# One more group of edges picked by matmul in a two-layer graph network, with its source table loaded earlier

## The chip, the core and the metric

The kernel runs on one core of one Trainium2 chip. The metric is the device time of one execution in microseconds (us); less is better. The engines named below are TensorE (PE, with its weight loads as PEld), VectorE (DVE), ScalarE (ACT), GpSimd (POOL) and SyncE (SP), which issues most of the transfers.

## What is computed

Two graph layers with a residual and a layer norm each, over 3125 nodes of 128 features and 100000 edges sorted by destination. Cut to what matters:

```python
edge_index = jnp.stack([src, dst])
x = layernorm(x + L0(x, edge_weight, src, dst, ...))
x = layernorm(x + L1(x, edge_index, ...))
# L0: msgs = z[dst] @ Wd + z[src] @ Ws + edge_weight * ww + bm
#     agg  = segment_max(msgs, dst);  hidden = relu(z @ W1a + agg @ W1b + b1);  out = hidden @ W2 + b2
# L1: two mean-aggregating layers: mean(x[src] over dst) @ Wl.T + bl + x @ Wr.T, relu between
```

The work around the change is the gather `z[src] @ Ws`, that is, for each edge one row of the table `zs = x @ Ws`, and the running maximum over the edges of one destination.

## The kernel before

The edges are cut into superbatches of 256 and the superbatches into 196 groups of two (512 edges). A loop over slots runs on all engines at once; group k enters in slot k, and its later steps are done in slots k+1 and k+2. A first stretch (about 40 us) loads the inputs, makes `zs` (stored to DRAM as `zs_d`) and the tables of keys.

In slot k, for a usual group:
- POOL runs `gathers(g)` ahead of the slots (line 1089): four indirect DMAs of 128 rows of `zs_d` each, into a ring of GR = 4 groups. Before it starts group g it waits until PE has transposed group g-4 (`t_ps`, line 1097), which frees the ring place.
- PE, `rows_T(g)` (line 1657): a matmul of nine rows for the weights of the edges (line 1663, it needs `wp_d`'s transfer of line 525), then four transposes of the gathered rows (line 1675, they need the gather's landing) into the same bank. Then `adjacent(k-2)` (lines 1724, 1727, 1735) and `products(k-1)` (line 1714).
- DVE: `scan` (line 1286), the running maximum with a mask that SP brings (line 528), and the one-hot tables of the two superbatches (lines 1269 to 1271).
- ACT: copies of the results into the adjacency table `adj` and into `aggT` (lines 896, 897) and of the transposed maxima (line 902).
- SP: `load_edges(k)` (line 521): the wp transfer after `t_ps` has reached k-1, the mask after scan k-2 is done (two buffers each), then four small row transfers of `own_rows` (line 586) and others. All of it is on one queue, in program order.

Twelve groups, PICKS, are not gathered: POOL skips them (line 1090), and PE forms their rows as a product of the whole source table with one-hot columns. For a pick (g, a) the 25 blocks h of the table are spread over slots a to g-1 (`hots`, line 129). For each h, `pick_rows` (line 1821) does two matmuls of 512 columns (line 1833), one for each of the two float32r parts, `zs_high` and `zs_low`. The one-hot columns of three blocks in four are made by ACT (lines 949 and 957), those of the fourth by DVE (line 1352). In its own slot the group needs the nine-row matmul alone (line 1661). The key row of a pick is loaded by SP in slot a-4 (`load_key`, line 588) and made float by ACT in slot a-2 (line 942).

The table itself is brought into SBUF once, in four pieces: `load_sources(n)` on SP in the slots SOURCE_SLOTS (three of 512 KB, line 602, and one of 26.5 KB, line 600), then `high_part` on ACT (line 938) and `low_part` on DVE (line 1345) in the slots that stand in SPLITS. The first pick before is group 28, worked on from slot 19.

Constants of the part that changes:

```python
PICKS = ((28, 19), (37, 28), (46, 37), (55, 46), (66, 55), (77, 66), (88, 77), (99, 88), (110, 99), (121, 110), (132, 121), (143, 132))
SPLITS = ((11, 0, 8), (13, 8, 16), (15, 16, 24), (16, 24, NT))
SOURCE_SLOTS = (8, 10, 12, 13)
```

Of the kernel before, what the change touches and what calls it, by code (L numbers as in the profile page):

```python
# [9 lines left out]
NT = -(-N // P)  # L10
# [37 lines left out]
MOST = 18  # L48
CR = 8
WIDE = 8  # L50
PICKS = ((28, 19), (37, 28), (46, 37), (55, 46), (66, 55), (77, 66), (88, 77), (99, 88), (110, 99), (121, 110), (132, 121), (143, 132))
PICKED = tuple(g for g, _ in PICKS)
SPLITS = ((11, 0, 8), (13, 8, 16), (15, 16, 24), (16, 24, NT))
SOURCE_SLOTS = (8, 10, 12, 13)
HOTS = 4
RAWS = 3
ROW = AW // 2
# [14 lines left out]
def turn(t):  # L72
    return NG if t == NT - 1 else last_group(t)
# [55 lines left out]
def hots(k):  # L129
    return [(i, h) for i, (g, a) in enumerate(PICKS) if a <= k < g  # L130
            for h in range(NT * (k - a) // (g - a), NT * (k - a + 1) // (g - a))]
# [22 lines left out]
def gnn_kernel(nc, x, src, dst, w, Wm, bm, W1, b1, W2, b2, W1lT, b1l, W1rT, W2lT, b2l, W2rT, out):  # L154
# [19 lines left out]
    with ctx:  # L174
# [3 lines left out]
        def sem(name):  # L178
            return ctx.enter_context(nc.semaphore(name))

        def carve(base, *shapes):

            at, views = 0, []
            for dt, *dims in shapes:
# [54 lines left out]
        zs_r = [nc.alloc_sbuf_tensor_at(f"zs_r{n}", [P, (h1 - h0) * ROW], f32r, offset=adj_at + 4 * h0 * ROW)[:, :]  # L239
                .rearrange("p (h n) -> p h n", n=ROW) for n, (_, h0, h1) in enumerate(SPLITS)]  # L240
        zs_high = [z[:, :, high_at:low_at] for z in zs_r]
# [134 lines left out]
        l_zs, zs_high_sb, zs_low_sb = sem("l_zs"), sem("zs_high_sb"), sem("zs_low_sb")  # L376
        l_part = [sem(f"l_part{n}") for n in range(len(SPLITS))]
        l_key, key_float = sem("l_key"), sem("key_float")
# [58 lines left out]
        def tiled(table, t, m):  # L437
            return table[t * P:(t + m) * P, :].rearrange("(t p) f -> p t f", p=P)
# [4 lines left out]
        def tiles(k, off, late=0):  # L443
            return [t for t in range(NT) if turn(t) + off + (late if t >= NT - 2 else 0) == k]
# [27 lines left out]
        def _(sp):  # L472
# [28 lines left out]
            for c in range(BB):  # L501
                n = BLAST if c == BB - 1 else P
# [18 lines left out]
            def load_edges(g):  # L521
                n, i = edges(g), g % MR
                if g >= WR:
                    sp.wait_ge(t_ps, g - WR + 1)
                sp.dma_start(wp9[:, g % WR, 0:n], wp_d[:, 512 * g:512 * g + n]).then_inc(l_wp[g % WR], 16)
                if g >= MR:
                    sp.wait_ge(scanned, g - MR + 1)
                sp.dma_start(mask[:, i, 0:n], mask_d[0:1, 512 * g:512 * g + n].broadcast_to([P, n])).then_inc(l_mask[i], 16)
# [9 lines left out]
            def usual():  # L538
                def load_quad(n, stored):
                    _, _, h0, h1, _ = PIECES[LOADS[n]]  # L540
                    if n >= 2:
                        sp.wait_ge(piece_ps, LOADS[n - 1])
                    sp.wait_ge(x1_st, 32 * stored)
                    sp.dma_start(quads[n % 2][:, 0:h1 - h0, :], tiled(parts_d, h0, h1 - h0)).then_inc(l_quad[n % 2], 16)

                def load_tile(t):
                    if t >= 2:
                        sp.wait_ge(y_sb, t - 1)
                    sp.dma_start(x_rows(t)[0:size(t), :], x[t * P:t * P + size(t), :]).then_inc(l_xr[t % 2], 16)

                def store_scale(j):
                    sp.wait_ge(scale_sb, j + 1)
                    n, w = strips(j)
                    rows = degree_rows(j)[0:32 * n:32, 0:w]
                    sp.dma_start(scale_d[0:1, span(j)[0]:span(j)[1]].rearrange("o (q c) -> (o q) c", c=w), rows).then_inc(scale_st, 16)

                def store_x1(t):
                    k = size(t)
                    sp.wait_ge(x1_sb, t + 1)
                    sp.dma_start(x1_d[t * P:t * P + k, :], hid(t)[0:k, :]).then_inc(x1_st, 16)  # L560
                    if t < NT - 2:
                        sp.wait_ge(parts_sb, t + 1)
                        sp.dma_start(parts_d[t * P:t * P + k, :], pt[0:k, :, :].rearrange("p a f -> p (a f)")).then_inc(x1_st, 16)

                def store_zr(t):
                    k = size(t)
                    sp.wait_ge(zr_sb, t + 1)
                    sp.dma_start(zr_d.rearrange("(a p) n -> p a n", p=P)[:, :, t * P:t * P + k], zr_of(t)[:, :, 0:k]).then_inc(zr_st, 16)
# [3 lines left out]
                def own_rows(k):  # L572
                    for i, g in enumerate(OWN):
                        at = (4 * g + 3) * P
                        if k == g - STEP - 2:
                            if i >= 2:
                                sp.wait_ge(t_ps, OWN[i - 2] + 1)
                            sp.dma_start(own_r[:, i % 2, 0:P], src[at:at + P].rearrange("(o e) -> o e", o=1)).then_inc(l_own_r, 16)
                        for r in range(max(0, (k - g + STEP) * ROWS), min(P, (k - g + STEP + 1) * ROWS)):
                            if r == 0:  # L580
                                sp.wait_ge(l_own_r, 16 * (i + 1))
                            if r % LOAD == 0:
                                nodes[:] = nc.values_load_multi_w_load_instructions(
                                    own_r[:, i % 2, r:r + LOAD], engines=[mybir.EngineType.SP], min_val=0, max_val=N - 1,
                                    skip_runtime_bounds_check_because=NODES)[1]
                            sp.dma_start(own[r:r + 1, i % 2, :], zs_d[bass.ds(nodes[r % LOAD], 1), :]).then_inc(l_own[i % 2], 16)

                def load_key(i):
                    g = PICKED[i]
                    if i >= 2:  # L590
                        sp.wait_ge(far_made, made_by(by_scalar, NT * (i - 1)))
                        sp.wait_ge(hot_vec, made_by(by_vector, NT * (i - 1)))
                    row = src[512 * g:512 * g + 512].rearrange("(o a e) -> o a e", o=1, e=P)
                    sp.dma_start(keys[i % 2].bitcast(i32), row.broadcast_to([P, 4, P])).then_inc(l_key, 16)

                def load_sources(n):
                    _, h0, h1 = SPLITS[n]
                    sp.wait_ge(wc_sb, 1)
                    if h1 == NT:
                        sp.dma_start(zs_raw[0:LASTN, h0, :], zs_d[h0 * P:N, :]).then_inc(l_part[n], 16)  # L600
                    else:
                        sp.dma_start(zs_raw[:, h0:h1, :], tiled(zs_d, h0, h1 - h0)).then_inc(l_part[n], 16)

                for k in range(NG + 5):
                    if 2 <= k < NG:
                        load_edges(k)
                    if k == 5:
                        sp.wait_ge(wp_st, 48 * (BB - 1))
                        sp.wait_ge(zs_st, 16 * NX)
                    if k in SOURCE_SLOTS:  # L610
                        load_sources(SOURCE_SLOTS.index(k))
                    for i, (g, a) in enumerate(PICKS):
                        if k == a - 4:
                            load_key(i)
                    own_rows(k)
                    for t in tiles(k, 0):
                        load_tile(t)
                    for t in tiles(k, 12):
                        store_x1(t)
                    for t in tiles(k, 16):  # L620
                        store_zr(t)
                    if k - 2 in DEGREE_SLOTS:
                        store_scale(DEGREE_SLOTS.index(k - 2))
                    for n, c in enumerate(LOADS):
                        if PIECES[c][0] - 1 == k:
                            load_quad(n, len([t for t in range(NT) if turn(t) + 12 <= k]))
# [185 lines left out]
        def _(act):  # L812
# [70 lines left out]
            def usual():  # L883
# [84 lines left out]
                for k in range(SLOTS):  # L968
# [7 lines left out]
                    if slots(k, 1) is not None:  # L976
                        messages(k - 1)
                    for n, (at, h0, h1) in enumerate(SPLITS):
                        if at == k:
                            high_part(n, h0, h1)  # L980
                    for i, (g, a) in enumerate(PICKS):
                        if k == a - 2:
# [182 lines left out]
        def _(dve):  # L1165
# [97 lines left out]
            def usual():  # L1263
# [90 lines left out]
                for k in range(SLOTS):  # L1354
# [23 lines left out]
                    if k - 1 in DEGREE_SLOTS[:6]:  # L1378
                        scale_from(DEGREE_SLOTS.index(k - 1))
                    for n, (at, h0, h1) in enumerate(SPLITS):  # L1380
                        if at == k:
# [223 lines left out]
        def _(pe):  # L1605
# [103 lines left out]
            def usual():  # L1709
# [111 lines left out]
                def pick_rows(i, h):  # L1821
                    u, n = NT * i + h, size(h)
                    if h == 0:
                        pe.wait_ge(zs_low_sb, len(SPLITS))
                        if i:
# [219 lines left out]
```

## Time and profile before

| | |
|---|---|
| median of 3 runs | 1096.47 us (1095.42 to 1099.88) |
| profiled execution | 1098.6 us, of which its span 1096.8 us |
| PE busy | 1020.9 us (93%) |
| DVE busy | 852.8 us (78%) |
| POOL busy | 739.7 us (67%), 701 gathers from `zs_d` among it |
| ACT busy | 671.0 us (61%) |
| mean granted TensorE clock | 0.98 |

Times in the views are microseconds from the start of the span. Busy times of POOL leave out the time in which it issues. The slots of the loop run from about 40 to 960 us; what follows (the second layer's aggregation) is PE work. Which slot a moment belongs to is read off PE: every slot k below 196 has one nine-row matmul, of line 1663, or of line 1661 where group k is picked.

### The profile page before, as it was taken

The numbers are of one execution on the slowest core, as the hardware profiler recorded it, in microseconds if no ns is written. First come the engines' busy times: TensorE is split into PE (matmuls) and PEld (weight loads), VectorE is DVE, ScalarE is ACT, GpSimd is POOL, SyncE is SP. The second block draws the span as 40 slices with busy tenths as digits, with TensorE's granted clock in tenths as the row PEclk, the third lists the DMA queues.
The fourth block names the chain that finished last, engine by engine and source line by source line (L and its number), as shares of the span: only waits on it lengthen the run. The fifth ranks groups of instructions, "written<-read, shape, count | busy, mean of one in ns | idle before, by whom it ended". The sixth has DMA issues, their size and how long they took to land.

```text
span 1096.8 us, 25699 instructions
## 1 busy us (share of the span) xinstructions
PE 1020.9 (93%) x7183; PEld 756.1 (69%) x7183; DVE 852.8 (78%) x2994; ACT 671.0 (61%) x1741; POOL 739.7 (67%) x782
## 2 busy tenths in 40 slices
PE   4898989999999999999999999998988989899997
PEld 4576667777777777776767777766666666657786
DVE  6598788888878878887979888987877877645465
ACT  3345778988887778877867887433233333313664
POOL 7767777777777777777777777777777777201332
PEclk9898999999999999999999999999999999999999
DMA  8654434344334434434444443543444353545321
GB/s 204 166 130 114 96 98 103 94 100 119 95 102 106 107 104 107 101 94 128 107 102 92 104 94 98 144 107 88 115 132 104 101 148 99 147 127 164 80 59 42
DMA packets 130203, 121.29 MB, mean 111 GB/s; under 512 B 24126, under 2 KB 115573, under 8 KB 130053
## 3 DMA queue, kind: packets, MB, share of 16 engines
q1 hardware_dynamic: 103624, 70.53, 24.5%
q0 software_dynamic: 23328, 47.82, 18.0%
q10 hardware_dynamic: 3101, 1.21, 0.5%
q8 instruction: 62, 1.02, 0.4%
q14 instruction: 88, 0.72, 0.3%
HBM read 105.60 MB, written 13.88 MB: 109 GB/s over the span
## 4 chain that ended last, share of the span: by engine, by line
PE 48%; POOL 27%; issue 13%; ACT 4%; DVE 3%; DMA 2%; ACTq 2%; DVEq 0%; SPq 0%
POOL area L1100 27%; PE bank L1833 9%; PE bank L1735 8%; PE bank L1959 7%; PE bank L1724 5%; PE bank L1802 4%; PE bank L1675 4%; PE bank L1714 3%; PE bank L1663 2%; PE bank L1924 2%; ACT area L949 1%; PE bank L1910 1%; DMA area<-zs_d,area 1%; ACT hot_r L957 1%; ACTq L889 1%
## 5 line engine op out<-in xcount | busy, mean ns | idle before, releaser
L1100 POOL DMA_INDIRECT area<-zs_d,area x701 | 679.7, 970 | 216.4 <-issue 210.9
L896 ACT CAST adj_w<-bank 128x325 f32 x391 | 176.6, 452 | 312.7 <-PE bank L1735 244.7
L1286 DVE TENSOR_TENSOR_SCAN area<-area,bank 128x512 f32<-128x512 bf16 x196 | 249.6, 1274 | 141.1 <-PE bank L1675 122.2
L1270 DVE TENSOR_SCALAR area<-area 128x325 bf16<-128x325 f16 x782 | 252.2, 323 | 0.0
L1735 PE MATMUL bank<-area 128*128 128x104 f32 x1564 | 225.1, 287 | 0.2
L1269 DVE TENSOR_SCALAR area<-area 128x128 bf16<-128x128 f16 x782 | 209.3, 268 | 5.4 <-PE bank L1735 5.3
L1735 PEld LDWEIGHTS bank<-area 128*128 128x128 f32 x1564 | 196.1, 197 | 10.6 <-issue 2.0
L1833 PE MATMUL bank<-hot_r,zs_r 128*128 128x512 f32 x600 | 176.1, 420 | 1.9 <-ACT hot_r L957 1.2
L1724 PE MATMUL bank<-area 128*128 128x325 bf16 x782 | 151.5, 307 | 9.8 <-DVE area L1271 5.4
L949 ACT ACTIVATE area<-adj_w,node_c 128x512 bf16<-128x512 f32 x225 | 156.5, 744 | 0.0
L1675 PE MATMUL bank<-ident,area 128*128 128x128 f32 x706 | 117.1, 289 | 27.5 <-DMA area<-zs_d,area 27.1
L957 ACT ACTIVATE hot_r<-area 128x512 fp32r<-128x512 bf16 x225 | 133.2, 639 | 1.1
L1675 PEld LDWEIGHTS bank<-ident,area 128*128 128x128 f32 x706 | 74.6, 141 | 70.1 <-DMA area<-zs_d,area 39.0
L1714 PE MATMUL bank<-ident,area 128*128 128x128 f32 x782 | 119.1, 275 | 2.2 <-DVE area L1286 2.2
L902 ACT COPY area<-bank 128x512 f32<-128x512 f32 x196 | 118.1, 602 | 4.3 <-PE bank L1714 4.2
L1833 PEld LDWEIGHTS bank<-hot_r,zs_r 128*128 128x128 f32 x600 | 102.1, 189 | 26.5 <-ACT hot_r L957 5.7
L1802 PE MATMUL bank<-adj_w,area 128*128 128x512 bf16 (+4 forms) x525 | 112.3, 354 | 5.3 <-issue 1.4
L1121 POOL CAST counts<-adj_w 128x512 fp32r<-128x512 bf16 (+2 forms) x45 | 28.7, 643 | 118.1 <-DVE area L1406 70.4
L1271 DVE TENSOR_SCALAR area<-area 128x25 bf16<-128x25 bf16 x391 | 96.3, 246 | 0.0
L1714 PEld LDWEIGHTS bank<-ident,area 128*128 128x128 f32 x782 | 93.8, 148 | 2.5 <-DVE area L1286 2.5
L1724 PEld LDWEIGHTS bank<-area 128*128 128x128 bf16 x782 | 61.3, 98 | 31.6 <-issue 10.8
L1802 PEld LDWEIGHTS bank<-adj_w,area 128*128 128x128 bf16 (+1 forms) x525 | 47.1, 98 | 51.8 <-issue 15.5
(175 smaller groups left out, 1105.9 us busy)
## 6 DMA issues: line engine op xcount, KB each, us to landing
area<-mask_d SPq DMA_DIRECT2D x195, 128.0 KB
area<-zs_d,area POOLq DMA_INDIRECT x701
area<-zs_d SPq DMA_DIRECT2D x640, 0.5 KB
area<-parts_d SPq DMA_DIRECT2D x20, 384.0 KB, 6.8
area<-wp_d SPq DMA_DIRECT2D x195, 9.0 KB
adj_w<-in_src_dram SPq DMA_DIRECT2D x12, 256.0 KB
zr_d<-area SPq DMA_DIRECT2D x24, 128.0 KB
area<-zr_d SPq DMA_DIRECT2D x6, 512.0 KB, 3.9
```

Source lines behind the costliest of these rows:

```text
L896: nc.scalar.copy(adj[:, :, bass.ds(at, W)], A_BANK[s % 2][:, 0:COLS].rearrange("p (h w) -> p h w", w=W))
L949: nc.scalar.activation(far[c % RAWS], keys[i % 2], ACT.Square, bias=node_c[:, h:h + 1], scale=-1.0).then_inc(far_made, 1)
L1100: pool.indirect_dma_start(gring[:, g % GR * 4 + s % 2 * 2 + u, :], None, x if g < RAW else zs_d[0:N, :], bass.IndirectOffsetOnAxis(ap=firs ...
L1269: nc.vector.tensor_scalar(hot_l[:, r, u, :], i_key[:, 0:P], lo_n[:, u, s:s + 1], None, ALU.is_equal)
L1270: nc.vector.tensor_scalar(hot_d[:, r, u, :], i_key[:, 0:COLS], key_n[:, u, s:s + 1], None, ALU.is_equal)
L1286: nc.vector.tensor_tensor_scan(S[:, g % 2, 0:n], mask[:, g % MR, 0:n], (G_BANK if g in PICKED else T_BANK[g % 2])[:, 0:n], S[:, (g + 1) % ...
L1675: last = nc.tensor.matmul(o[:, b * P:(b + 1) * P], rows, ident[:, :], start=False, stop=b == n // P - 1, is_transpose=True)
L1714: last = nc.tensor.transpose(S_BANK[:, b * P:(b + 1) * P], S[:, g % 2, b * P:(b + 1) * P], ident[:, :])
L1724: last = nc.tensor.matmul(o[:, 0:COLS], hot_l[:, r, u, :], hot_d[:, r, u, :], start=u == 0, stop=u == 1 and s == 0)
L1735: last = nc.tensor.matmul(o[:, 384:384 + WIDE * W].rearrange("p (n w) -> p n w", w=W), St[:, b * P:(b + 1) * P], sel[:, g % 2, u, s % 2, : ...
L1802: last = nc.tensor.matmul(o[:, 0:b - a], row[0:k, i * F:(i + 1) * F], adj[0:k, h, a:b], start=start and i == 0, stop=stop and i == 2)
L1833: last = nc.tensor.matmul(G_BANK.rearrange("p (a e) -> p a e", e=P), part_of[0:n, h - SPLITS[at][1], :], hot_r[u % HOTS][0:n], start=h == ...
```

## The change

A pick (19, 10) is put ahead of the twelve: group 19 is no longer gathered, and PE forms its rows in slots 10 to 18. For that the table has to be there earlier: pieces 0 and 1 are loaded in slot 5, piece 2 in slot 6, the small piece 3 in slot 7 (before: slots 8, 10, 12 and 13), and they are split in slots 6, 7, 8 and 9 (before: 11, 13, 15 and 16). The new pick's key row is loaded in slot 6 and made float in slot 8. As two pieces are loaded in one slot now, the loop on SP is written to allow it.

```diff
-PICKS = ((28, 19), (37, 28), (46, 37), (55, 46), (66, 55), ...
+PICKS = ((19, 10), (28, 19), (37, 28), (46, 37), (55, 46), (66, 55), ...
 PICKED = tuple(g for g, _ in PICKS)
-SPLITS = ((11, 0, 8), (13, 8, 16), (15, 16, 24), (16, 24, NT))
-SOURCE_SLOTS = (8, 10, 12, 13)
+SPLITS = ((6, 0, 8), (7, 8, 16), (8, 16, 24), (9, 24, NT))
+SOURCE_SLOTS = (5, 5, 6, 7)
...
-                    if k in SOURCE_SLOTS:
-                        load_sources(SOURCE_SLOTS.index(k))
+                    for n, at in enumerate(SOURCE_SLOTS):
+                        if at == k:
+                            load_sources(n)
```

## Rows read from the trace of the kernel before

**Rows 1.** The page's costliest groups: count | busy, mean ns | idle before, releaser.
```profile
L1100 POOL DMA_INDIRECT area<-zs_d,area x701 | 679.7, 970 | 216.4 <-issue 210.9
```
**Rows 2.** POOL's waits at 60 to 200 and at 200 to 660: total, times, longest.
```profile
POOL area L1100 <- PE bank L1675: 3.1, 1, 3.1
...
POOL area L1100 <- PE bank L1675: 2.1, 7, 0.3
```
**Rows 3.** The chain that ended last, in order of time: start, us, what.
```profile
65.03 0.60 PE bank L1675 x4
...
66.31 0.94 POOL area L1100
...
188.95 3.79 DMA area<-zs_d,area
...
655.77 0.94 POOL area L1100
```
**Rows 4.** PE's waits for gathered rows at 60 to 200 and at 200 to 660.
```profile
PE bank L1675 <- DMA area<-zs_d,area: 6.9, 8, 1.8
...
PE bank L1675 <- DMA area<-zs_d,area: 1.2, 1, 1.2
```
**Rows 5.** PE in order of time, slots 7, 11, 19, 20, 28, 34 and 35.
```profile
64.65 0.38 PE L1663 MATMUL bank<-area,ww 9*128 9x512 bf16 x1
...
78.40 0.39 PE L1663 MATMUL bank<-area,ww 9*128 9x512 bf16 x1 [1.95 <-DMA area<-wp_d]
...
115.04 0.38 PE L1663 MATMUL bank<-area,ww 9*128 9x512 bf16 x1
...
123.93 1.67 PE L1833 MATMUL bank<-hot_r,zs_r 128*128 128x512 f32 x6
...
160.64 0.39 PE L1661 MATMUL bank<-area,ww 9*128 9x512 bf16 x1
...
186.33 0.38 PE L1663 MATMUL bank<-area,ww 9*128 9x512 bf16 x1
...
192.78 0.66 PE L1675 MATMUL bank<-ident,area 128*128 128x128 f32 x4 [0.89 <-DMA area<-zs_d,area]
```
**Rows 6.** Stretches: length, busy of PE, PEld, DVE, ACT, POOL, clock, DMA share, GB/s.
```profile
60.00:80.00 20.00, 18.05 (x139) 13.99 (x138) 18.81 (x72) 9.05 (x30) 13.12 (x14) 1.00 0.57 140
80.00:100.00 20.00, 18.05 (x108) 14.51 (x108) 17.38 (x56) 8.97 (x26) 15.42 (x15) 0.76 0.53 128
100.00:120.00 20.00, 17.42 (x103) 13.06 (x101) 17.91 (x69) 13.23 (x35) 15.28 (x16) 0.82 0.36 86
...
160.00:180.00 20.00, 20.00 (x138) 15.42 (x138) 16.73 (x58) 19.02 (x48) 15.12 (x17) 1.00 0.48 108
```
**Rows 7.** SP's queue in order of time, slots 5 to 7: wp (L525), mask (L528).
```profile
53.93 0.35 SPq L528 DMA_DIRECT2D area<-mask_d  x1
56.05 0.27 SPq L525 DMA_DIRECT2D area<-wp_d  x1
57.30 0.35 SPq L528 DMA_DIRECT2D area<-mask_d  x1
...
61.34 0.28 SPq L525 DMA_DIRECT2D area<-wp_d  x1
```
**Rows 8.** 512 KB loads: three back to back at the start; then the table's, apart.
```profile
L475 SPq DMA_DIRECT2D adj_w<-in_x_dram x3: 422/582/1497, 1.2 to 2.3; - x3
DMA to landing us min/median/max: 4.7/7.2/12.1
...
adj_w<-zs_d SPq DMA_DIRECT2D x3, 512.0 KB, 5.5
```
**Rows 9.** Lines of DVE: duration in ns min/median/max, first and last start, forms.
```profile
L1345 DVE TENSOR_TENSOR zs_r<-adj_w,zs_r x4: 273/1225/1225, 84.1 to 106.7; 128x1024 fp32r<-128x1024 f32 x3, 53x128 fp32r<-53x128 f32 x1
...
L1352 DVE TENSOR_SCALAR hot_r<-adj_w,node_c x75: 471/476/671, 119.7 to 685.8; 128x512 fp32r<-128x512 f32 x75
```

**Rows 10.** POOL in order of time: the first gather of group 15, the 17th from 66.31.
```profile
86.47 0.95 POOL L1100 DMA_INDIRECT area<-zs_d,area  x1 [0.30 <-issue]
```

More of the change, by code:

```diff
@@ L50 @@
 WIDE = 8
-PICKS = ((28, 19), (37, 28), (46, 37), (55, 46), (66, 55), (77, 66), (88, 77), (99, 88), (110, 99), (121, 110), (132, 121), (143, 132))
+PICKS = ((19, 10), (28, 19), (37, 28), (46, 37), (55, 46), (66, 55), (77, 66), (88, 77), (99, 88), (110, 99), (121, 110), (132, 121), (143, 132))
 PICKED = tuple(g for g, _ in PICKS)
-SPLITS = ((11, 0, 8), (13, 8, 16), (15, 16, 24), (16, 24, NT))
-SOURCE_SLOTS = (8, 10, 12, 13)
+SPLITS = ((6, 0, 8), (7, 8, 16), (8, 16, 24), (9, 24, NT))
+SOURCE_SLOTS = (5, 5, 6, 7)
 HOTS = 4
```

## The prediction

> **What bounds the kernel now.** I read the totals first, then who waits for whom, then the chain in order of time, and last single slots. By busy time PE leads, but a gather also costs POOL the time in which it issues: 679.7 us busy and 210.9 us of issue for 701 gathers [rows 1] make 1.27 us each, 5.1 us for a group of four. POOL has almost no other idle time: from 60 us to the last gather it waited for PE for 3.1 us once, and up to 660 us for another 2.1 in seven short waits [rows 2]. So from 66.31 us on [rows 3] POOL runs through to the end of the gathers as if nothing stood in its way. The chain shows where PE joins it. It runs along POOL from 66.31, where POOL had waited for the transposes of group 7 at 65.03 to free a ring place, to 188.95, where PE waits for landed rows; then along PE, and back to POOL at 655.77 [rows 3]. In between PE waited only 1.2 us for rows [rows 4] and POOL at most 0.3 us at a time [rows 2]: the two are balanced there. Before that, PE waited 6.9 us for rows in eight waits [rows 4], all of them in slots 19 to 35 (the last is the one at 192.78, in slot 35 [rows 5]); after 655 us it is POOL's chain again.
>
> Three consequences. A group taken off POOL is worth 5.1 us and no more, since the rest of POOL's run has no waits to give back. The gain reaches the end only if PE is also earlier when its own stretch begins, at about 193 us. And whatever delays PE's transposes of group 7 delays POOL one for one, as that is the one place where POOL stands still for long.
>
> **The change part by part.** *Four gathers less.* POOL skips group 19, at about 107 us by its pace from 66.31 on: 4 x 1.27 = -5.1 us for every later gather [rows 1]. This has one answer.
>
> *The table's loads, earlier.* SP issues them on the queue that also feeds the slots, in program order: pieces 0 and 1 go behind the mask of slot 5 (issued at 53.93), ahead of the wp transfer of slot 6 (56.05); piece 2 and the pick's key row (256 KB) behind the mask of slot 6 (57.30), ahead of four own-row transfers and the wp transfer of slot 7 (61.34) [rows 7]. Before, they were issued apart and landed 5.5 us later [rows 8], when PE still had several groups gathered ahead of it. Now 1 MB stands ahead of wp 6 and another 0.75 MB ahead of wp 7. The nearest rows are the three loads of the same size at the start, issued back to back: they landed after 4.7, 7.2 and 12.1 us [rows 8], the first two about 2.9 us apart counting their issue spacing of 0.4 us. By that spacing, pieces 0 and 1, issued at 54.3 and 54.7, land at about 59.3 and 62.1, piece 2 at 65.0, the key row, half as large, at 66.4, and wp 7 at 66.7. PE wanted wp 7 at 64.65 [rows 5], so the transposes of group 7, and with them POOL, are 2.1 us late. The lower bound is 0: piece 2, issued at about 57.7, lands in 5.5 us as it did alone, at 63.2, in time. The upper bound is 5.2 us: it lands in 12.1 us, as the third of the three at the start did, at 69.8. I take 2.1, from the two loads that had the least beside them. POOL's account is then -5.1 + 2.1 = -3.0 us (ends -5.1 and +0.1).
>
> The Trainium skill, page "DMA: Bandwidth & Descriptors", section "Queues, rings and completion order", says that each DMA engine takes the descriptors of one ring in order, so a small transfer of SP stands behind SP's large ones. That speaks against this part of the change; by it the 2.1 us stand. If a small transfer could pass a large one, the term would be 0 and POOL's account -5.1 us. No row of the kernel before shows a small transfer of the loop issued right behind a large one.
>
> *The splits, earlier.* DVE does three of 1.225 us and one of 0.27, 3.95 us in all [rows 9], and waits for ACT's halves. They leave slots 11 to 16 and go to slots 6 to 9. There DVE is the fullest engine, 18.81 us of 20 [rows 6], so nothing hides them: the one-hots come later by that much, and PE's `adjacent` waits for them. ACT (9.05 of 20 us in the same stretch) hides its part. POOL is not touched by this, as the transposes of group 7 stand ahead of it and later ones have more room: the gathers of group 15, for example, started at 86.47 [rows 10], 7 us after their place was free (slot 11 began at 78.40, and its transposes were over about 1 us later [rows 5]).
>
> *The pick itself.* 25 blocks x 2 matmuls at 1.67/6 = 0.28 us [rows 5] add 14.0 us to PE in slots 10 to 18, less 0.6 us for the four transposes of group 19. What a slot with such a pick costs when nothing is waited for is read off slots 28 to 34: (186.33 - 160.64)/6 = 4.28 us [rows 5]; ACT is full there too, 19.02 of 20 us [rows 6], and the pick is as dense (25 blocks in nine slots). I take 4.4, for the tile work that falls into some slots. DVE's six extra one-hots, 0.48 us each [rows 9], are in that pace.
>
> *PE's account.* Slot 11 began at 78.40, of which 1.95 us were a wait for wp [rows 5], which I put down to the loads of slots 8 and 10 on its queue; they are gone from there. New: 78.40 - 1.95 + 2.1 (feed) + 3.95 (splits) = 82.5. Eight slots at 4.4 bring slot 19 to 117.7, against 115.04: 2.7 us late. The waits for rows of slots 19 to 35 are not needed then: 2.7 - 6.9 = -4.2 us at slot 35, against the -3.0 us at which the rows can be there. So POOL would decide, with 1.2 us to spare.
>
> *The clock.* The granted clock was 0.76 at 80 to 100 us and 0.82 at 100 to 120 [rows 6], that is half speed (1.2 GHz) for 2 x (0.24 + 0.18) x 20 = 16.8 us, which cost PE 8.4 us of full-speed work; it fell after PE had stood still, as it did before 78.40 [rows 5]. Before, this was hidden, since PE had groups in hand and then waited anyway. Now PE has no more than 1.2 us to spare. With the pick's matmuls it stands still less in slots 10 to 18, but still in slots 6 to 9, behind the feed and DVE. The cost lies between 0 and 8.4 us; I take a quarter, 2.1, since four of the slots 6 to 18 in which it can fall keep their idle time. That makes PE's account -4.2 + 2.1 = -2.1 us, which is now the later of the two, and the forecast. PE's stretch to 655 us has no slack, nor has POOL in it [rows 2, 3], so the -2.1 us go through to the end.
>
> The profiled execution took 1098.6 us (span 1096.8, 1.8 around it), 2.1 above the median of the runs. Its sum is 1098.6 - 2.1 = 1096.5; on the median's scale 1096.47 - 2.1 = 1094.4 us.
>
> **The rivals.** *The feed is hidden.* wp 7 is in time, because the small transfers are not held up or the loads overlap better; PE's account gains the same 2.1 us, POOL decides, and all 5.1 us are gained: 1091.4 us. For it: 0.57 of the DMA engines' time in that stretch [rows 6]. Against: the back-to-back loads at the start.
>
> *PE becomes the bound from slot 10 on.* Place: slots 10 to 18; price: the full half-speed time, 8.4 us, on top of the -4.2, so +4.2 us, 1100.7 us; with the feed at its upper end, 3.1 us more, 1103.8. It decides from the point where slot 19 begins over 6.9 us late (after 121.9 us), since then the waits of slots 19 to 35 no longer absorb it. For it: DVE, ACT and PE are all near full there. Against: the pace of 4.28 us in an equal stretch at full clock.
>
> *It does not take the group off what ends last.* PE is late enough in slots 14 to 18 that POOL waits for a ring place, and the 5.1 us go into that wait: no change, 1096.5 us. POOL had some 7 us of room at group 15 [rows 10], and slot 11 at 82.5 is 4.1 us late.
>
> **How the numbers follow.** Forecast (between -3.0 and -1): 0.5. Feed hidden, -5.1: 0.2. No change: 0.15. PE the bound, +4.2 or more: 0.15. A measurement of this kernel can tell about 0.5% from no change, 5.5 us here, and the greatest gain that the rows allow, 5.1, is under that. So faster by more needs the feed-hidden case and luck of the runs, half of its 0.2: 0.1. Slower by more needs the upper part of the PE case, and of a feed as late as its bound: 0.12. The rest, 0.78, is within 0.5%. The range goes from the full gain, with 1 us for the spread of the runs, 1090.4, to PE's case with some of the late feed, 1101.5.
>
> **What would show it.** Right: in the profile after, 697 gathers; POOL's long wait near 66 us grown by about 2 us and its later run without waits; PE waiting for wp in slots 6 and 7; slot 11 at about 82 to 85 us and slot 19 at 117 to 121; almost no waits for rows between slots 20 and 35; the last gather about 2 us earlier. The feed step is wrong if PE finds wp 6 and 7 landed, the split step if `adjacent` doesn't wait for DVE in slots 8 to 10, the clock step if the granted clock between 60 and 120 us is 1.00 or as low as before. The whole would be wrong if POOL waits for ring places after slot 20, or if the gathers' pace of 1.27 us changes.

## The result, and the profile after

The changed kernel takes 1105.52 us (median of 6 runs, 1102.29 to 1107.29); the kernel before, run beside it, 1098.07 (1095.42 to 1099.88). The ratio is 1.0053 with an interval of 1.0037 to 1.0068: some 5.8 us slower, and above the range that was given (the two medians by themselves are 7.5 us apart, the upper end of that interval). A later repeat gave 1.0036 (1.0023 to 1.0049), so the loss is 4 to 6 us. The profiled execution took 1106.67 us, its span 1104.9.

The chain's shares by engine on the page of the kernel before, then on that of the changed kernel, with its gathers on POOL (count | busy, mean ns | idle before):

```profile
PE 48%; POOL 27%; issue 13%; ACT 4%; DVE 3%; DMA 2%; ACTq 2%; DVEq 0%; SPq 0%
```
```profile
PE 55%; POOL 13%; issue 12%; ACT 7%; DVE 6%; DMA 4%; ACTq 2%; SPq 0%; DVEq 0%
...
L1101 POOL DMA_INDIRECT area<-zs_d,area x697 | 675.2, 969 | 226.3 <-issue 206.4
```

The four gathers are gone and a gather's pace is unchanged, 1.27 us as in [rows 1]. But the chain that ended last runs along POOL for 13% only, where it was 27% before; PE, ACT and DVE have taken its place. POOL's own waits say the same (POOL at 60 to 200 and at 200 to 660 us: total, times, longest; it answers to [rows 2]):

```profile
POOL area L1101 <- PE bank L1676: 7.2, 5, 5.1
...
POOL area L1101 <- PE bank L1676: 11.1, 10, 4.4
```

Before, these were 3.1 and 2.1 us. POOL now stands still for 13.1 us more and issues 5.1 us less; it has become the engine that waits. For PE the wait for rows of [rows 4] is missing altogether in both stretches. Its waits at 60 to 200 us are now these:

```profile
PE bank L1725 <- ACT area L898: 2.9, 5, 1.6
PE bank L1725 <- DVE area L1272: 2.8, 3, 1.3
PE bank L1664 <- DMA area<-wp_d: 2.6, 3, 1.2
```

PE had no wait for ACT at 60 to 200 us before.

The starts of slots 7, 11, 12, 19, 20, 27, 28 and 35, from the changed kernel's PE in order of time (they answer to [rows 5]):

```profile
66.74 0.38 PE L1664 MATMUL bank<-area,ww 9*128 9x512 bf16 x1 [1.15 <-DMA area<-wp_d]
...
83.60 0.38 PE L1664 MATMUL bank<-area,ww 9*128 9x512 bf16 x1
...
89.32 0.39 PE L1664 MATMUL bank<-area,ww 9*128 9x512 bf16 x1
...
120.93 0.38 PE L1662 MATMUL bank<-area,ww 9*128 9x512 bf16 x1
...
127.81 0.57 PE L1664 MATMUL bank<-area,ww 9*128 9x512 bf16 x1
...
159.14 0.39 PE L1664 MATMUL bank<-area,ww 9*128 9x512 bf16 x1
...
165.53 0.39 PE L1662 MATMUL bank<-area,ww 9*128 9x512 bf16 x1
...
195.79 0.38 PE L1664 MATMUL bank<-area,ww 9*128 9x512 bf16 x1
```

And of the kernel before, slots 12, 20, 27 and 35, beside those in [rows 5]:

```profile
82.43 0.60 PE L1663 MATMUL bank<-area,ww 9*128 9x512 bf16 x1
...
119.35 0.38 PE L1663 MATMUL bank<-area,ww 9*128 9x512 bf16 x1
...
156.06 0.38 PE L1663 MATMUL bank<-area,ww 9*128 9x512 bf16 x1
...
191.51 0.38 PE L1663 MATMUL bank<-area,ww 9*128 9x512 bf16 x1
```

Slot 7 is 2.1 us late against before, slot 11 5.2, slot 19 5.9, slot 20 8.5, slot 28 4.9 and slot 35 4.3 (0.34 us of each was there at slot 3 already, ahead of any part of the change). Three slots stand out by their length: slot 11 takes 5.7 us, slot 19 6.9 and slot 27 6.4, where they took 4.0, 4.3 and 4.6 before. The chain of the changed kernel, in order of time, goes through slot 19 like this (start, us, what):

```profile
118.42 0.64 ACT hot_r L958
119.06 0.52 ACTq L890
119.58 2.49 issue
...
123.53 0.44 PE bank L1725 x2
```

Line 890 (889 before) stands in `adjacent`: every 16th tile, that is every eighth slot, ACT loads the next 16 start columns into its registers before it can copy. ACT in order of time shows the pause in the changed kernel, three times:

```profile
84.22 0.46 ACT L897 CAST adj_w<-bank 128x325 f32 x1 [2.59 <-issue]
...
122.20 0.46 ACT L897 CAST adj_w<-bank 128x325 f32 x1 [2.62 <-issue]
...
160.20 0.46 ACT L897 CAST adj_w<-bank 128x325 f32 x1 [2.64 <-issue]
```

They end in slots 11, 19 and 27, the three long ones. The kernel before has the same loads. Grouped by the source line, with count, then ns min/median/max and first to last start, before and after:

```profile
L889 ACTq TENSOR_LOAD <-area x25: 1547/3447/3658, 45.8 to 937.2; - x25
```
```profile
L890 ACTq TENSOR_LOAD <-area x25: 1552/3447/3629, 46.2 to 945.0; - x25
```

The difference lies in what ACT had around them. Its waits at 84 to 122 us, first before, then after (total, times, longest):

```profile
ACT adj_w L896 <- PE bank L1735: 15.1, 10, 4.5
```
```profile
ACT adj_w L897 <- issue: 2.6, 1, 2.6
...
ACT adj_w L897 <- PE bank L1736: 0.4, 1, 0.4
```

Before, ACT waited 15.1 us for PE there, and a load that ran in such a wait cost nothing. The load of slot 18, for example, ran from 110.05 to 113.48 us before, and the copy behind it still had to wait for PE (ACT in order of time, before):

```profile
113.86 0.46 ACT L896 CAST adj_w<-bank 128x325 f32 x1 [2.70 <-PE bank L1735]
```

The pick's one-hots on ACT fill that time, so the same load is now a stop that PE feels.

### The profile page after: what moved, and what is told of

Its sections match the earlier page's. It is cut to its first block, busy times and chain, and to the rows that moved or that the text cites. A ratio compares the mean times of both kernels' runs of the same rounds, so it can differ in the third digit from the quotient of the medians.

```text
span 1104.9 us, 25849 instructions
## 1 busy us (share of the span) xinstructions
PE 1025.2 (93%) x7199; PEld 760.5 (69%) x7229; DVE 854.2 (77%) x3000; ACT 690.8 (63%) x1780; POOL 734.8 (67%) x778
## 3 DMA queue, kind: packets, MB, share of 16 engines
q10 hardware_dynamic: 3101, 1.21, 0.4%
## 4 chain that ended last, share of the span: by engine, by line
PE 55%; POOL 13%; issue 12%; ACT 7%; DVE 6%; DMA 4%; ACTq 2%; SPq 0%; DVEq 0%
POOL area L1101 13%; PE bank L1834 10%; PE bank L1736 9%; PE bank L1960 7%; PE bank L1725 6%; PE bank L1676 5%; PE bank L1803 4%; PE bank L1715 4%; PE bank L1664 3%; ACT area L950 2%; ACT hot_r L958 2%; ACTq L890 1%; ACT area L903 1%; DVE area L1287 1%; PE bank L1925 1%
## 5 line engine op out<-in xcount | busy, mean ns | idle before, releaser
L1736 PE MATMUL bank<-area 128*128 128x104 f32 x1564 | 222.1, 284 | 0.3
L1736 PEld LDWEIGHTS bank<-area 128*128 128x128 f32 x1564 | 193.0, 194 | 10.9 <-issue 2.7
L1834 PE MATMUL bank<-hot_r,zs_r 128*128 128x512 f32 (+1 forms) x650 | 191.7, 421 | 1.4 <-ACT hot_r L958 0.8
L950 ACT ACTIVATE area<-adj_w,node_c 128x512 bf16<-128x512 f32 x244 | 169.6, 744 | 0.0
L958 ACT ACTIVATE hot_r<-area 128x512 fp32r<-128x512 bf16 x244 | 144.4, 639 | 1.2
L1834 PEld LDWEIGHTS bank<-hot_r,zs_r 128*128 128x128 f32 (+1 forms) x650 | 111.4, 191 | 28.0 <-ACT hot_r L958 7.0
L1803 PE MATMUL bank<-adj_w,area 128*128 128x512 bf16 (+4 forms) x495 | 106.0, 353 | 10.4 <-issue 3.3
```

The source lines that it names most:

```text
L950: nc.scalar.activation(far[c % RAWS], keys[i % 2], ACT.Square, bias=node_c[:, h:h + 1], scale=-1.0).then_inc(far_made, 1)
L1736: last = nc.tensor.matmul(o[:, 384:384 + WIDE * W].rearrange("p (n w) -> p n w", w=W), St[:, b * P:(b + 1) * P], sel[:, g % 2, u, s % 2, : ...
L1803: last = nc.tensor.matmul(o[:, 0:b - a], row[0:k, i * F:(i + 1) * F], adj[0:k, h, a:b], start=start and i == 0, stop=stop and i == 2)
L1834: last = nc.tensor.matmul(G_BANK.rearrange("p (a e) -> p a e", e=P), part_of[0:n, h - SPLITS[at][1], :], hot_r[u % HOTS][0:n], start=h == ...
```

## The experiments

The first four kernels set two theories against each other. A: ACT is full in slots 10 to 18, and its register loads, which had cover before, now stand on the path. B: the table's earlier loads and splits are what costs the time. C, that the pick's 14 us of matmuls on PE are enough to explain it, whatever ACT does, is put against A in the second kernel and in the four that follow. The last runs turn A's suspect, the length of one load, up and down. Ratios are against the kernel before, timed beside each.

**The earlier table alone**, in the kernel before (with the change's loop on SP):

```diff
-SPLITS = ((11, 0, 8), (13, 8, 16), (15, 16, 24), (16, 24, NT))
-SOURCE_SLOTS = (8, 10, 12, 13)
+SPLITS = ((6, 0, 8), (7, 8, 16), (8, 16, 24), (9, 24, NT))
+SOURCE_SLOTS = (5, 5, 6, 7)
```

> The twelve picks of before, with the table loaded in slots 5 to 7 and split in slots 6 to 9 as in the changed kernel; group 19 is gathered again. Theory A (the table's early loads hold up wp on SP's queue by 2.1 us at slot 7, which POOL inherits; the rest of the loss comes from the pick's work in slots 10 to 19): POOL's wait near 66 us is 5.1 us as in the changed kernel, PE catches up with POOL again by slot 35, and the time is before + 2.1 us, ratio about 1.002. Rival B (the early loads and splits are themselves the loss, by slot 11 all of its 5.2 us): before + 5 to 7 us, ratio about 1.005.

Measured: 1100.69 against 1099.68 us, 1.0007 (0.9991 to 1.0022). PE still waited 7.7 us for rows in eight waits at 60 to 200 us, and only 0.3 us for `wp`. PE in this kernel, slots 11 and 18:

```profile
83.60 0.39 PE L1664 MATMUL bank<-area,ww 9*128 9x512 bf16 x1
...
109.43 0.39 PE L1664 MATMUL bank<-area,ww 9*128 9x512 bf16 x1
```

Slot 11 begins at the same 83.60 us as in the changed kernel (1.6 us of its lateness was there at slot 3 already, ahead of the early loads), but slot 18 begins 0.5 us ahead of the kernel before (109.94), where the changed kernel is 6.0 us late (115.96). B falls: without the pick, loads and splits this early cost at most 2.4 us by the interval, because PE's waits for rows behind them are still there to take the delay. What was expected of the feed was too much here: from slot 4 to slot 7 PE took 10.32 us against 10.13 before. The pick's key row of slot 6 isn't in this kernel. POOL's long wait was the expected 5.0 us, but it isn't a sign of the feed by itself: the kernel before with short loads (below), whose table is not early, shows 4.9, as its slot 4 began 1.9 us late.

**No register loads**, in the changed kernel and in the one before. Both kernels copy to fixed columns, so the start columns are not read, and the windows stand near their true columns, not at them (shortened; the two copies lose their `bass.ds` as well):

```diff
-if s % RC == 0:
-    starts[:] = nc.values_load_multi_w_load_instructions(...)[1]
-at = starts[s % RC]
+at = s * N // NS
...
-adj[:, :, bass.ds(at, W)]
+adj[:, :, at:at + W]
```

> The changed kernel without ACT's loads of the starts into registers (every eighth slot, 2.5 us of ACT each): the windows of the adjacency table are written at fixed columns near the true ones, so that part of the computation is changed. Theory A (PE is the bound from slot 7 on, and the three register loads of slots 10, 18 and 26, hidden before behind PE's waits for rows, now stand on its path, as do later ones): PE is ahead of POOL again, POOL decides, and the time is before - 5.1 + 2.1 = about -3 us, ratio about 0.997. Rival C (the pick's 14 us on PE are the loss by themselves, ACT's loads are hidden): within 1 us of the changed kernel, ratio about 1.005.

> The kernel before with the same part left out (no loads of the starts into registers, fixed columns). Theory A: POOL runs through without waits there, so work taken off ACT and PE gives nothing: before - 1 us to before, ratio 0.999 to 1.000. Rival D (PE's stretch of 195 to 655 us decides by itself, and each register load on its chain is worth 2.5 us): 20 us less, ratio about 0.98.

Measured: 1095.42 us, 0.996 (0.9942 to 0.9978), for the changed kernel without them, and 1096.63, 0.9975 (0.9959 to 0.9992), for the one before. Without the loads the change no longer costs time, with them it is a loss. The loads cost the changed kernel 0.8 to 0.9% (from 1.0036 or 1.0053) and the one before about 0.25%, more than was expected of the latter, but nowhere near the 20 us of D. PE, changed kernel without loads, slot 35, and PE's waits for rows at 200 to 660 us:

```profile
190.13 0.38 PE L1660 MATMUL bank<-area,ww 9*128 9x512 bf16 x1
```
```profile
PE bank L1672 <- DMA area<-zs_d,area: 6.8, 8, 1.4
```

Slot 35 begins 1.4 us before its time in the kernel before (191.51), instead of 4.3 after, and PE waits for rows again: POOL decides once more.

**The table's loads on ACT's queue**, changed kernel: the same loads, issued by ACT at the same slots.

```diff
-                            load_sources(n)      # in SP's loop over the slots
+                            load_sources(n)      # in ACT's loop over the slots
-                        sp.dma_start(zs_raw[:, h0:h1, :], tiled(zs_d, h0, h1 - h0)).then_inc(l_part[n], 16)
+                        act.dma_start(zs_raw[:, h0:h1, :], tiled(zs_d, h0, h1 - h0)).then_inc(l_part[n], 16)
```

> The changed kernel with the four loads of the table issued from ACT's queue in the same slots, so that SP's small transfers have none of them ahead. Theory A: PE does not wait for wp in slots 6 and 7, slot 7 begins at 64.7 instead of 66.7, POOL's wait is 3.1 us again, and PE's path to slot 35 starts 2.1 us earlier: the changed kernel - 2 us, ratio to before about 1.003. If the transfers are held up on the engines whatever queue they come from: as the changed kernel, 1.005.

Measured: 1108.62 us, 1.0082 (1.0055 to 1.0109), no better than the changed kernel. SP now issues the `wp` transfer of slot 7 at 62.68 us, not at 65.13, and PE waits for it all the same. SP's queue, then PE, then the DMA queues at 64 to 66 us (packets, MB, share of 16 engines), in this kernel:

```profile
62.68 0.28 SPq L525 DMA_DIRECT2D area<-wp_d  x1
```
```profile
68.46 0.60 PE L1663 MATMUL bank<-area,ww 9*128 9x512 bf16 x1 [3.46 <-DMA area<-wp_d]
```
```profile
q10 hardware_dynamic: 1070, 0.54, 93.4%
...
q1 hardware_dynamic: 2, 0.00, 0.2%
```

So the expected gain missed. The order on SP's queue isn't quite clear of large transfers here, as the pick's 256 KB key row, issued at 57.98, is still ahead of `wp`. But the key row's packets were all moved by 64 us, and in the next two SP's queue (q1) moved 2 packets with `wp` outstanding, while ACT's (q10, which has 6275 packets in this kernel and 3101 in the changed one) took 93.4% of the engines' time. So a small transfer is held up also by large ones of another engine's queue. The total doesn't tell more: ACT reached the three large loads 2.7 to 3.6 us later than SP had (58.29, 58.74 and 61.67 against 54.73, 55.17 and 58.94), so the table itself came later too.

**The changed kernel again**, beside the next three, with no edit.

> The changed kernel itself once more, as the yardstick for the three beside it on the same chip. Both theories: ratio to before 1.004 to 1.007.

Measured: 1103.58 against 1100.21 us, 1.0036 (1.0023 to 1.0049). Slot 19 began at 121.81 us, slot 35 at 195.54, and POOL waited 13.5 us for PE at 200 to 660 us. These are the values to hold the next three against.

**More of the pick on DVE.** Every second one-hot of the first pick goes to DVE, not every fourth: 6 fewer on ACT, 6 x (0.744 + 0.639) = 8.3 us by the page's means of their two lines.

```diff
-    return u % 4 == 3
+    return u % 2 == 1 if u < NT else u % 4 == 3
```

> The changed kernel with 12 instead of 6 of the first pick's 25 one-hot blocks made by DVE; six blocks of 1.28 us leave ACT, six of 0.48 us are added to DVE in slots 10 to 18. Theory A (ACT, without a pause from 84 to 122 us in the changed kernel, sets the pace of slots 10 to 19 together with its register and table loads): slot 19 begins 3 us earlier or more, and the time is the changed kernel - 2 to - 4 us, ratio to before about 1.003. Rival C (PE's 14 us set it): the changed kernel within 1 us, 1.005 to 1.006.

Measured: 1101.05 us, 1.0012 (0.9997 to 1.0028), 2.5 us better than the repeat. ACT at 84 to 122 us and slot 19 in this kernel:

```profile
ACT adj_w L897 <- PE bank L1736: 3.5, 5, 1.1
```
```profile
119.16 0.39 PE L1662 MATMUL bank<-area,ww 9*128 9x512 bf16 x1
```

ACT waits for PE again, slot 19 begins 2.6 us earlier than in the repeat (1.1 of it was there at slot 4; 3 or more were expected), and POOL's wait for PE at 200 to 660 us falls from 13.5 to 5.9 us. No matmul was taken away, so by C nothing should have moved.

**One matmul for two.** The first pick multiplies by the high part of the table alone; the low part is left out for group 19, which takes 7 us off PE.

```diff
-for part_of in (zs_high[at], zs_low[at]):
+for part_of in (zs_high[at], zs_low[at]) if i else (zs_high[at],):
```

> The changed kernel with the first pick done by one matmul for each block instead of two (the product with the low part of the table is left out for group 19 alone): 7.0 us less on PE in slots 10 to 18, ACT as it was. Rival C (PE alone sets the pace there): slot 19 begins up to 7 us earlier and PE waits for rows again, the time is the changed kernel - 5 us or better, ratio about 1.000. Theory A (ACT sets it at least as much): the changed kernel - 0 to - 2 us, ratio 1.004 to 1.006.

Measured: 1102.99 us, 1.0023 (1.0012 to 1.0035). Of the 7 us only 0.6 (medians) to 1.4 (ratios) come back. Slot 19 begins at 121.18, and ACT at 84 to 122 us has no wait for PE:

```profile
ACT adj_w L897 <- issue: 5.2, 2, 2.6
```

C falls as the cause by itself: with 7 us less PE work ACT is still full, and sets the pace; PE now waits 2.7 us for ACT's one-hots at 60 to 200 us, where it was 0.2.

**The key row early.** The first pick's 256 KB key row is loaded in slot 3, not in slot 6.

```diff
+                    sp.wait_ge(wc_sb, 1)         # in load_key, ahead of the transfer
...
-                        if k == a - 4:
+                        if k == (a - 4 if i else 3):
```

> The changed kernel with the first pick's key row (256 KB) loaded in slot 3, ahead of the table, instead of slot 6 behind it. Theory A (of the 2.1 us that slot 7 is late, some 1.5 come from the key row behind three loads, whose issue SP held for 1.8 us): wp of slot 7 is issued about 1.5 us earlier, slot 7 begins at about 65.2, POOL's wait near 66 us is about 3.6 us, and the time is the changed kernel - 1.5 us, ratio about 1.004. If the three loads alone hold the queue: as the changed kernel.

Measured: 1104.94 us, 1.0037 (1.0023 to 1.0052), as the repeat. PE's wait for `wp` in slot 6 fell to 0.6 us and there is no other, against 2.6 us in three waits in the changed kernel, so the key row is a good part of the late feed: from slot 4 to slot 7 PE took 10.76 us here, 11.88 in the changed kernel, 11.52 in the repeat and 10.13 before. The 1.5 us that were expected at the end don't come, for the splits hold PE in slot 8, and so all that follows. From slot 4 to slot 10 it is 23.46 us here, 23.35 in the changed kernel and 23.02 with the earlier table alone, against 18.85 before: feed and splits overlap, and the splits end last (PE in order of time, the waits of slots 6 and 8 in brackets):

```profile
63.65 0.39 PE L1665 MATMUL bank<-area,ww 9*128 9x512 bf16 x1 [0.56 <-DMA area<-wp_d]
...
73.58 0.46 PE L1726 MATMUL bank<-area 128*128 128x325 bf16 x2 [1.82 <-DVE area L1273]
```

**Longer loads.** The constant `RC` is the number of starts that one load brings in. With 32 there are half as many loads, each twice as long. The third kernel also has more of the pick on DVE.

```diff
-RC = 16
+RC = 32
```

> The changed kernel with ACT's starts loaded 32 at a time, every 16th slot, instead of 16 every eighth: the loads of slots 10, 26, 42 and so on are gone, those of slots 18, 34, 50 stay and grow by about a third. Theory A (each register load stands on ACT's full path): slot 11 begins 2 us earlier, half of what the kernel without register loads gained comes back, the time is the changed kernel - 3 to - 5 us, ratio to before about 1.000. If a load of 32 costs twice one of 16: as the changed kernel, 1.004.

> The kernel before with the same larger register loads. Theory A (POOL decides there, and the kernel before without any register load was 0.25% faster): ratio 0.998 to 1.000. If ACT's loads decided there too: 0.995 or less.

> The changed kernel with both reliefs of ACT: register loads of 32, and 12 instead of 6 of the first pick's one-hot blocks on DVE. Theory A: slot 19 begins less than 2 us late against before, the waits of slots 19 to 35 absorb it, POOL decides again, and the thirteenth pick brings part of its 5.1 us: ratio to before 0.996 to 0.999. If the pick's loss has another cause than ACT's time: 1.001 or more, as with the one relief alone.

Measured: 1119.15 us, 1.0184 (1.016 to 1.0208), for the changed kernel; 1116.66, 1.0166 (1.0137 to 1.0196), for the one before; 1115.83, 1.0153 (1.0129 to 1.0177), with more on DVE. The changed kernel's loads, by their line:

```profile
L890 ACTq TENSOR_LOAD <-area x13: 1546/6857/7000, 46.3 to 959.7; - x13
```

All three expectations missed (about 1.000 or 1.004, 0.998 to 1.000, 0.996 to 0.999): a load of 32 takes twice as long as one of 16, not a third more, and does more than twice the harm. The length of one load, not their total, makes the time: 13 of 6.86 us do more harm than 25 of 3.45. The kernel before lost nearly as much, as its waits for rows do not cover a stop of 6.9 us. At 60 to 660 us PE waited 22.8 us for ACT, and POOL 30.4 for PE:

```profile
PE bank L1724 <- ACT area L897: 22.8, 12, 4.6
```
```profile
POOL area L1100 <- PE bank L1675: 30.4, 18, 4.8
```

The clock has a part in it. The granted clock of this kernel's six runs was 0.966 in the mean, against 0.980 beside it; at 320 to 360 us of the profile it was 0.91 against 1.00, that is 2 x 0.09 x 40 = 7.2 us at half speed (1.2 GHz), in a stretch where PE's busy time fell from 38.77 to 35.37 us. How much of the 17 to 20 us is standing still and how much is clock was not separated.

**Shorter loads**, `RC = 4`: the changed kernel, the one before, and the changed one with more on DVE.

> The changed kernel with ACT's starts loaded four at a time, every other slot, instead of 16 every eighth; the traces show 3.45 us for 16 and 6.85 for 32, so about 0.9 us each and the same total. If single long loads are what ACT's schedule can't absorb (theory A, narrowed): PE's waits of 1.5 us for ACT near slots 11, 20 and 27 go, the time is the changed kernel - 4 us or better, ratio to before 0.996 to 1.000. If the total of ACT's time is the cause: as the changed kernel, 1.004 to 1.005.

> The kernel before with the same smaller register loads. POOL decides there, and leaving the loads out altogether gave 0.25%: ratio 0.997 to 1.000.

> The changed kernel with register loads of four and 12 instead of 6 of the first pick's one-hot blocks on DVE. Theory A, narrowed: slot 19 begins less than 4 us late, the waits of slots 19 to 35 absorb it, POOL decides from there on: ratio to before 0.995 to 0.998, better than either kernel. If ACT's total is the cause: as with the relief by DVE alone, 1.001.

Measured: 1095.48 against 1099.78 us, 0.9961 (0.9946 to 0.9975); 1097.04, 0.9974 (0.9965 to 0.9983); 1096.87, 0.9965 (0.9952 to 0.9977). The changed kernel with short loads is faster than both kernels of the case. Its loads, slot 35 on PE, and POOL's waits and PE's waits for rows at 200 to 660 us:

```profile
L890 ACTq TENSOR_LOAD <-area x98: 700/913/1235, 45.5 to 942.6; - x98
```
```profile
189.23 0.38 PE L1664 MATMUL bank<-area,ww 9*128 9x512 bf16 x1
```
```profile
POOL area L1101 <- PE bank L1676: 2.1, 7, 0.3
```
```profile
PE bank L1676 <- DMA area<-zs_d,area: 7.3, 7, 1.6
```

The total is about the same, 98 x 0.91 = 89 us against 25 x 3.45 = 86, but PE has enough in hand to run on through 0.9 us: it has no wait for ACT's copies at 60 to 660 us, where it had 2.9 and 7.0 us in the two stretches with loads of 16. Slot 35 begins 2.3 us earlier than before the change (0.6 of it was there at slot 3 already), POOL's long waits at 200 to 660 us are gone, and PE waits for rows again, as it did in [rows 4]. With short loads ACT has no long stop, and moving more of the pick to DVE brings nothing: the same edit that gave 2.5 us with loads of 16.

The two pairs agree. Without loads the ratio goes from 0.9975 to 0.996 by the change, with short loads from 0.9974 to 0.9961: a gain of about 0.14%, 1.5 us, though the intervals of each pair overlap, so the gain itself is not shown. With loads of 16 it goes from 1 to 1.0053 (1.0036 in the repeat). So the change costs its 4 to 6 us only through the long loads; they take 8 to 10 us from the changed kernel (1.0036 or 1.0053, less 0.9961) and 2.9 from the one before (1 - 0.9974).

## Why the prediction was wrong

**The signs.** Slot 11 at 83.60 us and slot 19 at 120.93 lie in the ranges that were given for a right prediction. Behind them it breaks: POOL waits for ring places after slot 20, which was to show that the whole is wrong, and the last gather begins at 943.65 us, 5.3 later than before (938.37) and not 2 earlier.

**Four gathers less, -5.1 us.** Right as a ceiling: 697 gathers at 1.27 us. The gain is what POOL lost again by waiting for PE. In the kernels with the pick, POOL's wait for PE at 200 to 660 us goes roughly with the time: 11.1 us in the changed kernel, 13.5 in the repeat, 5.9 with more on DVE, 2.1 with short loads.

**The feed, +2.1 us.** Right in place, and near in size: slot 7 moved from 64.65 to 66.74, of which 1.75 us came after slot 4 (1.4 in the repeat). POOL's long wait grew from 3.1 to 5.1 us (POOL in order of time, after):

```profile
68.41 1.10 POOL L1101 DMA_INDIRECT area<-zs_d,area  x1 [5.14 <-PE bank L1676]
```

That the size came out is in part luck. By the rows that it names the landings would be 59.0, 61.9 and 64.8, 0.2 to 0.3 us ahead of what it says, and the main reason is another one. SP's own issue was held: the changed kernel's SP queue shows 1.76 us for `wp` of slot 6 and 1.81 for the key row, where [rows 7] has 0.27, so `wp` of slot 7 was issued at 65.13, not 61.34, and PE had it 1.6 us after that:

```profile
56.33 1.76 SPq L525 DMA_DIRECT2D area<-wp_d  x1
...
59.58 1.81 SPq L594 DMA_DIRECT2D adj_w<-in_src_dram  x1
...
65.13 0.28 SPq L525 DMA_DIRECT2D area<-wp_d  x1
```

And with the loads on ACT's queue the small transfer was late as well. The rule of the Trainium skill, page "DMA: Bandwidth & Descriptors", section "Queues, rings and completion order", that the descriptors of one ring are taken in order, gave the right sign here. But order in one ring isn't the whole of it: that kernel's `wp` of slot 7 stood in a queue without the table's loads, PE waited 3.46 us for it, and at 64 to 66 us, with `wp` issued, the other queue's packets filled the engines. Which shared part holds a small transfer back was not measured.

**The splits, +3.95 us.** Right in place: PE waited for DVE 2.8 us in three waits, and slot 11 began at 83.60 against the 82.5 of the sum. But feed and splits don't add, as the early key row showed.

**The pick itself and PE's account.** Here it failed. The step took 4.4 us for a slot, from 4.28 in slots 28 to 34, and said that ACT is full there too. Slots 11 to 18 took (120.93 - 83.60) / 8 = 4.67 us each, and slot 19 took 6.9. ACT's register loads have no term in the sum at all. The six slots that I measured hold no register load: the loads stand in every eighth slot, and the one of slot 26 ends in slot 27, just ahead of the first of them. So the pace was right for a slot without a load and was used for a stretch with one every eighth. It also looked at ACT's busy time, which does not count the loads: 19.02 of 20 us in [rows 6] was already a full engine, and 3.45 us more every eighth slot had no place in it. The 6.9 us of waits for rows [rows 4], which I spent once, also paid for these loads before: of the 8.5 us that slot 20 was late, slots 20 to 35 gave back only 8.5 - 4.3 = 4.2, and the load in slot 27 took 1.8 of what the waits gave. So from the -4.2 us at slot 35 to the measured +4.3 it goes in four steps: 1.1 us up to slot 11, 2.1 for the pace of slots 11 to 18, 2.6 for the length of slot 19, and 2.7 of the 6.9 that were not given back. The experiments show that the last three hang on the register loads: with the loads left out slots 11 to 18 took 4.45 us each, slot 19 3.4, and slots 20 to 35 gave back 5.5; with short loads it was 4.52, 3.4 and 5.5.

**The clock, +2.1 us.** Wrong in place, and no part of the cause. In the changed kernel's stretches (the columns of [rows 6]) the granted clock is 1.00 where I charged it, in slots 6 to 18:

```profile
80.00:100.00 20.00, 18.61 (x123) 14.00 (x124) 16.58 (x62) 16.72 (x41) 15.19 (x16) 1.00 0.39 100
100.00:120.00 20.00, 19.86 (x135) 15.19 (x134) 17.86 (x67) 18.35 (x42) 15.36 (x16) 1.00 0.35 87
...
120.00:140.00 20.00, 18.22 (x113) 13.47 (x112) 13.66 (x48) 15.86 (x41) 15.13 (x17) 0.91 0.37 89
```

PE is busier there than in [rows 6], and ACT went from 8.97 and 13.23 us to 16.72 and 18.35. The clock fell to half speed (1.2 GHz) later, from about 125 to 128 us, after PE had stood still for ACT's load in slot 19: 0.91 of 20 us is 2 x 0.09 x 20 = 3.6 us at half speed, 1.8 us of full-speed work. That is a part of slot 19's 6.9 us. It isn't needed for the result: in the repeat, with the same load, the clock was 1.00 in all five stretches from 60 to 160 us, slot 19 still took 5.9 us, and the kernel was still slower than before.

**The rivals.** The second, PE as the bound from slot 10 on, had the place. That its +4.2 us, forecast for the whole time (1100.7 us), is also the 4.28 measured at slot 35 is luck. Its price was wrong in kind: it was the half-speed clock there, and it is ACT here. Nor was its point of decision right: slot 19 began at 120.93, ahead of the 121.9 that it gave, and still lost, as the waits behind it had been spent on the loads. The feed hidden (1091.4) did not happen. The rival without change had POOL waiting for ring places, which is what it does, but later and for longer.

**What stays open.** After slot 35 the lateness in the one profiled execution goes between 1.8 and 6 us up to slot 155 and between 2.5 and 8.4 behind it, and is 7.5 at the last slot; where each part of this comes from wasn't followed. Executions differ too: slot 4 began at 54.5 us before, 54.9 after and 56.1 with the earlier table alone, so a difference of 1 us at one slot isn't evidence by itself.

## What to carry to other kernels

A wait on the path hides more than the thing that ends it: before filling it with work, list every periodic stop of each engine (register loads, table switches, queue issues) that now falls in it, and price each as if the wait were gone. Read a pace off a stretch that holds one whole period, and don't take busy time for fullness, since loads of registers aren't in it. Where a periodic load can't be removed, make it short and frequent: what the neighbour has in hand must outlast one of them, not their sum.

## What the runs showed of the hardware

The time of a register load on ACT is close to linear in what it brings in, 0.21 to 0.23 us each: 0.91 us for 4, 3.45 for 16, 6.86 for 32. SP's issue of a small transfer, 0.27 us by itself, took 1.76 us behind 1 MB of loads just issued. A third 512 KB load on ACT's queue took 2.37 us to issue, the first 0.41. With the table's loads on ACT's queue PE waited 3.46 us for a 9 KB transfer of SP's queue, against 1.15 with the loads on SP's; at 64 to 66 us, with that transfer issued, SP's queue moved 2 packets, and ACT's took 93.4% of the engines' time.
